# A softplus chain in a graph network kernel: the cap moves to GpSimd, the maxima one round later

## What is computed

```python
def ssp(x):
    return softplus(x) - log(2.0)

def _residual(m, W1, b1, W2, b2):
    y = ssp(m)
    h = ssp(y @ W1.T + b1)
    return m + h @ W2.T + b2

message = xi + xj                       # xj: the sum over the edges
for k in range(3):
    message = _residual(message, Wri1[k], bri1[k], Wri2[k], bri2[k])
message = ssp(message)
x = u * x + message @ Wd.T + bd
for k in range(2):
    x = _residual(x, Wra1[k], bra1[k], Wra2[k], bra2[k])
```

## Time and profile before

| | us |
|---|---|
| median of 3 runs | 8159.97 |
| lowest and highest run | 8117.99, 8174.51 |
| profiled execution | given by its span: 6637.6 |
| median less that span | 1522.4 |
| phase of the change in the trace | from about 4074 to 4284 |

### The profile page before, as it was taken

The page is one execution under the profiler, slowest core; times in us unless marked ns, Lnnn a source line. Parts: engine busy times, 40 slices in busy tenths (PEclk is TensorE's granted clock), DMA queues, the critical chain, the costliest instruction groups (busy, mean ns, idle before and its releaser), DMA issues. The chain is left out here.

```text
span 6637.6 us, 102436 instructions
## 1 busy us (share of the span) xinstructions
PE 4423.8 (67%) x25123; PEld 3459.8 (52%) x25123; DVE 4380.1 (66%) x14473; ACT 2606.2 (39%) x7316; POOL 4142.0 (62%) x4980
## 2 busy tenths in 40 slices
PE   7777777405555554655666666667777766999987
PEld 6566666304444443544555554345555554677665
DVE  7677777544444445776445446868888876877777
ACT  2355555203333334873000004734344434544443
POOL 0577777526777775455777772047777752777774
PEclk9987888755555556986666667888888886877887
DMA  1255555592111113632333331023333321333332
GB/s 66 64 150 154 150 149 149 118 51 51 54 54 54 54 54 102 162 89 69 79 80 79 80 79 24 3 65 79 79 79 79 80 56 49 77 74 74 75 74 54
DMA packets 834365, 533.67 MB, mean 80 GB/s; under 512 B 588596, under 2 KB 741000, under 8 KB 833416
## 3 DMA queue, kind: packets, MB, share of 16 engines
q1 hardware_dynamic: 702152, 261.57, 18.2%
q0 software_dynamic: 131648, 265.56, 14.6%
HBM read 399.11 MB, written 127.68 MB: 79 GB/s over the span
## 5 line engine op out<-in xcount | busy, mean ns | idle before, releaser
L1386 POOL DMA_INDIRECT l2e_rows<-l_rows,columns x832 | 793.1, 953 | 601.2 <-POOLq L226 348.0
L1386 POOL DMA_INDIRECT spare<-l_rows,k_dst_of x784 | 741.2, 945 | 385.6 <-issue 238.0
L1252 POOL DMA_INDIRECT dst_rows<-l0d_out,l0d_idx x832 | 802.1, 964 | 271.6 <-issue 239.7
L1386 POOL DMA_INDIRECT table<-l_rows,k_dst_of x784 | 743.2, 948 | 296.2 <-issue 238.7
L849 POOL DMA_INDIRECT src_records<-sort_rec,sort_idx x784 | 766.0, 977 | 241.0 <-issue 232.3
L1211 PE MATMUL l0d_pX<-table,l0d_ohT 128*128 x1664 | 457.9, 455 | 44.7 <-ACT l0d_ohT L1229 12.5
L2250 PE MATMUL l2e_pV<-l2e_rows,ident 128*128 128x512 f32 x416 | 273.9, 745 | 315.0 <-DMA l2e_rows<-l_rows,columns 311.0
L1201 PE MATMUL l0d_pT<-identb,l0d_oh 128*128 128x128 bf16 x832 | 124.8, 304 | 496.2 <-DVE l0d_oh L1177 496.2
L1624 DVE TENSOR_TENSOR l1e_prod<-l1e_pG,table 128x512 f32<-128x512 f32 x196 | 135.6, 692 | 480.8 <-issue 466.2
L1211 PEld LDWEIGHTS l0d_pX<-table,l0d_ohT 128*128 128x128 f32 x1664 | 390.2, 324 | 97.9 <-issue 97.8
L1594 PE MATMUL l1e_pG<-k_weights,table 64*128 64x128 f32 x1568 | 205.7, 398 | 346.9 <-DVE l1e_prod L1624 344.4
(11 more groups left out here) (414 smaller groups left out, 13251.5 us busy)
## 6 DMA issues: line engine op xcount, KB each, us to landing
l0m_rows<-dst_rows SPq DMA_DIRECT2D x196, 264.0 KB, 2.9
sort_rows<-lo_rows SPq DMA_DIRECT2D x196, 256.0 KB
sort_rec<-rec SPq DMA_DIRECT2D x98, 472.0 KB
l2e_lrow<-dst_local SPq DMA_DIRECT2D x208, 128.0 KB
table<-src_records SPq DMA_DIRECT2D x196, 128.0 KB
table<-src_records SPq DMA_DIRECT2D x196, 100.0 KB
dst_rows<-l0d_out,l0d_idx POOLq DMA_INDIRECT x832
l2e_rows<-l_rows,columns POOLq DMA_INDIRECT x832
```

The costliest lines, as they stand in the source:

```text
L1252: e.indirect_dma_start(kn.by_dst[:, :], bass.IndirectOffsetOnAxis(ap=r["idx"][:, st.quad, j:j + 1], axis=0), r["out"][:, st.quad, j, :], N ...
L1386: e.indirect_dma_start(r["rows"][:, i % ring, j, 0:width], None, table[:, :], bass.IndirectOffsetOnAxis(ap=columns[:, i * G + j:i * G + j ...
```

## The change

GpSimd gets a stream of its own in this phase. In update layers it makes the cap, as a minimum of the state with a column or with 20, in SBUF; ACT's Relu is gone, and its exponential takes the bias column in its place. For tiles 1, 3 and 5 of the six update layers that have a softplus (18 tiles), GpSimd also writes max(x - cap, 0), the excess, to the output tile, and later adds the logarithm to it, which takes the place of DVE's maximum. The other tiles' maxima stay on DVE. All closings come in round i+3 (`LATE = 3`) where the maxima came in round i+2. Waits for `maxed` are divided between the two counters `maxed` and `gmaxed` (`wait_maxed`). The layer with `Wd` names its bias. The number of banks (4) and of `part` buffers (4) is unchanged.

```diff
+LATE = 3
@@
+    caps = [i for i in softs if layers[i // NW].into is not None]
+    maxed = {"vector": [i for i in softs if i not in caps or i % NW % 2 == 0], "gpsimd": [i for i in caps if i % NW % 2]}
@@
+        def wait_maxed(e, i):
+            name = "vector" if i in maxed["vector"] else "gpsimd"
+            e.wait_ge(r["maxed" if name == "vector" else "gmaxed"], upto(maxed[name], i))
+
+        def smooth(e, i):
+            lay = layers[i // NW]
+            e.wait_ge(r["logged"], upto(softs, i))
+            e.scalar_tensor_tensor(wide(kn, lay.out, i % NW), seen(i), column(lay.less, -LN2), part(i), ALU.add, ALU.max
+                                   ).then_inc(r["maxed"], 1)
@@ tensor
-                    e.wait_ge(r["maxed"], upto(softs, i - NW))
+                    wait_maxed(e, i - NW)
@@
-                        e.wait_ge(r["maxed"], upto(softs, k))
+                        wait_maxed(e, k)
@@ vector
-            for i in range(n + 2):
+            for i in range(n + LATE):
@@
-                        e.wait_ge(r["maxed"], upto(softs, i - 4))
+                        wait_maxed(e, i - 4)
@@
-                j = i - 2
-                if j >= 0 and layers[j // NW].out is not None:
-                    old = layers[j // NW]
-                    e.wait_ge(r["logged"], upto(softs, j))
-                    e.scalar_tensor_tensor(wide(kn, old.out, j % NW), seen(j), column(old.less, -LN2), part(j), ALU.add, ALU.max
-                                           ).then_inc(r["maxed"], 1)
+                if i - LATE in maxed["vector"]:
+                    smooth(e, i - LATE)
@@ scalar
-                if i < len(softs) and lay.into is not None:
-                    e.wait_ge(r["updated"], upto(updates, i))
-                    if i > 3:
-                        e.wait_ge(r["maxed"], i - 3)
-                    ch(e.activation(part(i), wide(kn, lay.y, i % NW), ACT.Relu, bias=column(lay.cap, kn.cap1[:, 0:1]),
-                                    scale=-1.0))
-                    clamped = ch.done
@@
-                        ch.until(clamped)
-                        ch(e.activation(part(i), part(i), ACT.Exp, bias=kn.cap1[:, 0:1], scale=-1.0))
+                        e.wait_ge(r["capped"], upto(caps, i))
+                        ch(e.activation(part(i), part(i), ACT.Exp, bias=column(lay.bias, kn.zero1[:, 0:1])))
@@ new
+        def gpsimd(e, ch):
+            excess = {}
+            e.wait_ge(r["made"], 1)
+            for i in range(len(softs) + LATE):
+                if i in caps:
+                    lay = layers[i // NW]
+                    e.wait_ge(r["updated"], upto(updates, i))
+                    if i > 3:
+                        wait_maxed(e, i - 4)
+                    e.tensor_scalar(part(i), wide(kn, lay.y, i % NW), column(lay.cap, CAP), None, ALU.min
+                                    ).then_inc(r["capped"], 1)
+                    if i in maxed["gpsimd"]:
+                        ch(e.tensor_scalar(wide(kn, lay.out, i % NW), wide(kn, lay.y, i % NW), column(lay.cap, CAP), 0.0,
+                                           ALU.subtract, ALU.max))
+                        excess[i] = ch.done
+                if i - LATE in maxed["gpsimd"]:
+                    out = wide(kn, layers[(i - LATE) // NW].out, (i - LATE) % NW)
+                    ch.until(excess[i - LATE])
+                    e.wait_ge(r["logged"], upto(softs, i - LATE))
+                    e.tensor_tensor(out, out, part(i - LATE), ALU.add).then_inc(r["gmaxed"], 1)
+            e.wait_ge(r["gmaxed"], len(maxed["gpsimd"]))
```

More of the change, by code:

```diff
@@ L1488, in vector @@
                     if i > 3:
-                        e.wait_ge(r["maxed"], upto(softs, i - 4))
+                        wait_maxed(e, i - 4)
                     e.tensor_scalar(part(i), seen(i), column(lay.bias, 0.0), CAP, ALU.add, ALU.min
                                     ).then_inc(r["clamped"], 1)
-                j = i - 2
-                if j >= 0 and layers[j // NW].out is not None:
-                    old = layers[j // NW]
-                    e.wait_ge(r["logged"], upto(softs, j))
-                    e.scalar_tensor_tensor(wide(kn, old.out, j % NW), seen(j), column(old.less, -LN2), part(j), ALU.add, ALU.max
-                                           ).then_inc(r["maxed"], 1)
-            e.wait_ge(r["maxed"], len(softs))
+                if i - LATE in maxed["vector"]:
+                    smooth(e, i - LATE)
+            e.wait_ge(r["maxed"], len(maxed["vector"]))
             if updates:
@@ L1506, in scalar @@
             for i in range(len(softs) + 1):
-                lay = layers[min(i, n - 1) // NW]
-                if i < len(softs) and lay.into is not None:
-                    e.wait_ge(r["updated"], upto(updates, i))
-                    if i > 3:
-                        e.wait_ge(r["maxed"], i - 3)
-                    ch(e.activation(part(i), wide(kn, lay.y, i % NW), ACT.Relu, bias=column(lay.cap, kn.cap1[:, 0:1]),
-                                    scale=-1.0))
-                    clamped = ch.done
                 if i:
@@ L1526, in scalar @@
                     done[i] = ch.done
-        return dict(tensor=tensor, vector=vector, scalar=scalar)
+        def gpsimd(e, ch):
[3 more added lines that the diff above has]
+                if i in caps:
+                    lay = layers[i // NW]
+                    e.wait_ge(r["updated"], upto(updates, i))
[13 more added lines that the diff above has]
+            e.wait_ge(r["gmaxed"], len(maxed["gpsimd"]))
+        return dict(tensor=tensor, vector=vector, scalar=scalar, gpsimd=gpsimd)
     phase(kn, name, build, psums=[("p", [P, 4, 2, BANK], F32)],
           sbufs=[("part", [P, 4, 2, SEC], F32), ("cols", [P, max(1, len(columns))], F32)],
-          sems=["made", "product", "updated", "clamped", "logged", "maxed"])
+          sems=["made", "product", "updated", "clamped", "capped", "logged", "maxed", "gmaxed"])
 def load_records(kn, e, r, column, width, used):
@@ L1648, in l1_layers @@
         lay.append(Layer(kn.MT, w=f"Wri2_{k}", src=kn.TB, into=kn.AC, plus=f"bri2_{k}", y=kn.AC))
-    lay.append(Layer(kn.TB, w="Wd", src=kn.MT, into=kn.Hn, scale="u", y=kn.Hn, less=5, cap=6))
+    lay.append(Layer(kn.TB, w="Wd", src=kn.MT, into=kn.Hn, scale="u", y=kn.Hn, bias="bd", less=5, cap=6))
     lay.append(Layer(kn.MT, w="Wra1_0", src=kn.TB, bias="bra1_0", less=3))
```

## The result

The changed kernel takes 8356.4 us (median of 4 runs, 8320.2 to 8371.8) against 8166.7 us: ratio 1.023, 95% interval 1.0199 to 1.0262. It is slower by about 190 us. The forecast was slower by 135 us, 8295, with a range that ended at 8345: the direction and the place were right, the size was too small and the result lies 11 us beyond the range. Of these 11 us, 7 come from the median of the kernel before, which a fourth run moved from 8160.0 to 8166.7; in the stage itself the forecast is 46 us short (+135 against +181). Runs come in two groups, in which the kernel before takes about 8125 to 8170 us or about 6640 us, and every ratio here is taken within one group.

A forecast was written before the change was run, and what follows sets the result against it. ACT bounds update rounds (2.80 us), DVE bias rounds (2.11). At low clock 51.9 + 3 x 61.8 + 86.4 + 24.7 = 348.4, less 207.9: +140, less 5: +135, so 8295 us, range 8225 to 8345.

The forecast's parts named there:

- Maximum, PE and clamp are now in series: In bias layers each late maximum, PE's tile and DVE's next clamp follow one another: 4.23 us per round, 5.72 at low clock.
- stalled round: A round whose PSUM bank a bias layer last used, so PE waits for the late maximum; 35 over five bias layers.
- So I take the low clock for the stalled rounds: PE, too idle in bias layers, drops to 1.2 GHz: the stage grows by 140 us, 135 after allowing some full-clock rounds.
- I take 1.76, the same operation, and 2.3 for the additions: GpSimd's prices in us per operation in update layers: ten one-input operations and three additions, 24.5 us per layer.
- rival (b): POOL and DVE block each other or one-input work costs 2.7 us: some 8 us more per update layer, 8340 or more; chance 0.10.
- The ports: In update layers DVE's 24 two-SBUF-input maxima contend with GpSimd: put at nothing, up to 3 us per layer in the range.
- whoever is first holds the port for its whole length: Skill's rule for a DVE instruction with two SBUF inputs beside GpSimd reading SBUF; 0 to 1.5 us per maximum.
- roughly line rate: The skill's speed for one-input work on GpSimd; at 0.95 us the sum would be some 3 us smaller per update layer.
- rival (c): PE and clamp wait in series, but POOL is cheap (0.95 us) and the clock full: 8200 us; chance 0.08.
- full-clock sum: Schedule of the stage with PE at full clock, pair by pair: clamp 0 at 29.3 us, in all +87.5 us.
- 1522 us lie around the span: Difference between the profiled span of 6637.6 us and the median of 8160.0, taken as lying outside the span and untouched.
- Rival (d): PE has its bank before DVE's maximum is done, update rounds fall to 2.11 us: -29 us, 8131; chance 0.03.

## Why the prediction was right in kind and wrong in size

- *"Maximum, PE and clamp are now in series"*: right. The stalled round is 5.72 us where PE's clock is low, the series alone costs 87 us (run with the maxima late and GpSimd idle), and taking it out of the changed kernel gives 88 us back.
- *"So I take the low clock for the stalled rounds"*: mostly right. The stage's clock is 0.68, and 22 of the 35 stalled rounds show the 3.5 us wait of the low clock; the other 13 had 1.9 to 3.3. From clamp 0 to the next update layer the forecast had 28.4 us, measured are 28.0, 28.3 and 27.9 (layers 1, 3, 5).
- *GpSimd's operations, "I take 1.76, the same operation, and 2.3 for the additions"*: this term failed. The row taken as "the same operation" was an add and multiply; its engine and type were the same and its shape nearly, and its 1635 ns held a wait of some 0.8 us for a DVE addition. Measured are 2.56 for the caps, 3.3 to 3.8 for the excesses and 2.08 for the additions, 34.4 us per update layer instead of 24.5. Of the 9.9 us more, the caps' own price makes 4.8, that of the excesses 4.4, the additions take off 0.7, and lengthening beside DVE's maxima adds 1.4. Clamp 0 of a bias layer came 34.5 us after the first update instead of 23.6 in the first pair, and 38.2 and 39.4 us instead of 33.6 in the next two. The pairs took 62.5, 66.6, 67.3 and 66.9 us (forecast 51.9 and three times 61.8), layers 6 to 8 103.4 (86.4), the last 22.3 (24.7): 389.0 against 348.4 at the low clock, 41 us more. Layers 6 to 8, where GpSimd works through two update layers, make 17 of them and the first pair 11.
- *The range*: rival (b), dearer operations of GpSimd, described what happened ("8340 or more") and got 0.10. Its price was 2.7 us per operation at 13 operations, 35 us; measured 34.4. The rival's own rule, 8 us of stage per layer for 10.5 us more of GpSimd, gives 6 x 7.5 = 45 us for the 9.9 us measured, and 343 + 45 = 388 for the stage of 389.0: the mechanism was right, and this one size was off. I bounded one-input work from 0.95 to 2.98 and then gave the upper end too little: both ends have been seen since, 0.94 for one pair of operations and 3.2 for another.
- *The ports*: put at nothing, and not quite nothing. Five of DVE's 24 maxima with two SBUF inputs took 1.8 us instead of 1.09, each begun 1.2 us into an addition of GpSimd. The other way round, 5 of the 35 caps without a column took 3.2 to 3.3 us instead of 2.45. GpSimd's lengthening sums to some 8 us in the stage, 1.4 us per update layer, within the 3 us that the range allowed. The rule that the prediction drew on, *"whoever is first holds the port for its whole length"*, fits to within 0.15 us where DVE was first, and where an addition of GpSimd was. It doesn't fit a cap or an excess: a maximum waited for its first 0.8 us or so alone.
- *One-input work at "roughly line rate"*, and the price of rival (c): one-input work took 0.94 us, next to the lower bound of 0.95, for add with multiply alone. Two sums with this bound don't follow from the order of operations that the full-clock sum uses. In it six one-input operations and two additions lie between 13.9 us and clamp 0, so that clamp 0 comes at 13.9 + 6 x 0.95 + 2 x 2.3 = 24.2 us. The prediction has 19.2 under (c) and "some 3 us smaller" (26.3) under the ports. Rival (c) was therefore priced some 5 us per pair too low; the forecast doesn't use it.
- *"1522 us lie around the span"*: wrong, but without effect on the sum: the stage is as long in both groups to within 2 us.
- Rival (d), a gain, is out: with GpSimd's work and the late maxima the six update layers that have a softplus took 22.2 to 52.8 us from their first update to the next layer's start, against 17.5 to 19.6 before. With the maxima on time and a quick operation on GpSimd a gain exists: the run with only the quick pair, which leaves the cap out, has 14.5 us per update layer.

## What to carry to other kernels

When the closing operation of a tile moves one round later, look up every ring that it frees. Here PE's 4 banks gave one round of slack that was 0.15 us short of being used up already, and the move put matmul and vector work in series at 4.2 to 5.7 us per tile instead of 2.1. Work taken off an engine that bounds a stage must be priced on the new engine by a row of the very same operation, and by one that ran alone: engine, type and shape don't fix the price, and the row used here was half waiting.

## What the runs showed of the hardware

- GpSimd, 128x896 fp32 tensor_scalar with constants: add and multiply 0.94 us alone, a single minimum or multiplication 2.45, subtract and max 3.21, add and min 3.20, min and multiply 3.20. The pair add and multiply is quicker than the single multiplication.
- GpSimd's quick instruction took 1.71 to 1.78 us, 0.8 us more, in the 31 of 42 caps of its run that began while a DVE maximum with both inputs in SBUF was running, some 0.16 us after its start. In the changed kernel, caps of 2.45 us begun 0.17 us after such a start took 3.22 us, and excesses of 3.21 us begun 0.35 to 0.42 us after it took 3.74 to 3.81.
- A DVE maximum with both inputs in SBUF that began 0.50 us into a cap of 2.44 us ended 1.87 us after the cap's start; begun 1.2 us in or later it took its usual 1.08 to 1.09 us. Begun 1.2 us into an addition of GpSimd of 2.07 us it took 1.8 us.
- A DVE minimum from SBUF to SBUF on 128x896 fp32 takes 0.62 us, the maximum with two SBUF inputs 1.09.
- PE's four 128x448 fp32 matmuls took 3.33 us in rounds of 5.72, where the clock was at its low level (0.50 from 5110 to 5124). One tile's four took 1.67 us (5084.73, clock 1.00 from 5084.5 to 5086.5) right behind the matmuls of four tiles in a row.
